# Eight token buffers instead of four, with seven of the eight token tiles made by GpSimd in the attention stage

## The reference

```
h = token_mixer(x)                          # embedding, attention in 192 features, MLP, 2 layernorms
h = h + attention(layernorm(h))             # 12 heads of 16, rms-normed q and k
h = h + soft_moe(layernorm(h))
# soft_moe, for each group of 64 tokens:
xn      = l2norm(x) * sqrt(192) * gamma_in            # the "tokens"
logits1 = xn @ phi.T                                  # 64 tokens x 128 slots
disp1   = softmax over the tokens;  comb1 = softmax over the 128 slots
slots   = disp1.T @ xn;  yn = l2norm(slots) * sqrt(192) * gamma2
# then slot means, second slots, second dispatch, 8 x 4 small MLPs, and back:
out     = comb1 @ out2
```

## Time and profile before

| | |
|---|---|
| runs | 577.52, 575.09, 577.10 us, median 577.1 |
| profiled execution | span 575.4 us from the first to the last instruction; the page gives no separate time for it |
| attention block ends, first slots begins | about 272.6 us |
| first slots ends, second slots begins | about 336.3 us |
| PE busy | 538.0 us, 93% of the span |
| DVE, ACT, POOL busy | 315.0, 257.0, 82.7 us |
| mean granted TensorE clock | 0.985 of full speed |

### The profile page before, as it was taken

One profiled execution on the slowest core, in us unless ns is written; L12 is line 12 of the kernel. 1 busy time (PEld: TensorE's weight loads), 2 busy tenths in 40 slices (PEclk: granted clock), 3 DMA queues, 4 the chain that ended last, 5 costly groups with the idle time before them and its releaser, 6 DMA issues. The chain is left out here.

```text
span 575.4 us, 13736 instructions
## 1 busy us (share of the span) xinstructions
PE 538.0 (93%) x5529; PEld 440.9 (77%) x5529; DVE 315.0 (55%) x738; ACT 257.0 (45%) x822; POOL 82.7 (14%) x128
## 2 busy tenths in 40 slices
PE   6999999999999999999777799999979999999997
PEld 5888888766556656667546565888869999999986
DVE  2348777766777676652235735366643434444343
ACT  1234345356655576543446637366652323323220
POOL 6380000011104321300341100000000000000000
PEclk9999999999999999999869999999999999999999
DMA  6180000000000000000910023000009999999833
GB/s 239 35 283 2 2 0 2 1 2 1 2 2 2 1 1 2 2 1 1 377 76 2 1 90 117 2 1 2 1 1 381 412 331 315 322 335 337 232 56 117
DMA packets 20722, 58.81 MB, mean 102 GB/s; under 512 B 3042, under 2 KB 9796, under 8 KB 20548
## 3 DMA queue, kind: packets, MB, share of 16 engines
q1 hardware_dynamic: 14756, 49.47, 23.2%
q0 software_dynamic: 1056, 4.33, 4.1%
q10 hardware_dynamic: 4848, 4.13, 2.5%
HBM read 53.21 MB, written 4.33 MB: 100 GB/s over the span
## 5 line engine op out<-in xcount | busy, mean ns | idle before, releaser
L2042 PE MATMUL banks<-slots_t,w 64*128 64x128 f32 x1536 | 94.1, 272 | 1.3 <-PEq L1737 1.1
L2042 PEld LDWEIGHTS banks<-slots_t,w 64*128 64x128 f32 x1536 | 92.6, 188 | 1.9 <-issue 1.6
L1138 DVE TENSOR_REDUCE qk<-banks 128x4 f32<-128x1024 f32 x48 | 58.8, 1226 | 39.5 <-PE banks L601 39.5
L2115 ACT ACTIVATE ex_gelu<-banks,b_sb 128x128 f32<-128x128 f32 x128 | 36.6, 369 | 90.6 <-PE banks L2042 90.6
L601 PE MATMUL banks<-qk_t 16*128 16x256 f32 x384 | 54.3, 400 | 2.6 <-DVE qk L1138 2.4
L608 PE MATMUL banks<-qk_t 17*128 17x256 f32 x384 | 54.4, 400 | 0.0
L2135 DVE SCALAR_TENSOR_TENSOR ex_act_t<-banks,b_sb,ex_gelu 128x128 f32<-128x128 f32 x128 | 36.0, 344 | 29.6 <-ACT ex_gelu L2115 29.6
L2073 PE MATMUL banks<-w,ex_act_t 64*128 64x192 f32 x512 | 49.5, 323 | 1.0 <-DVE ex_act_t L2135 1.0
L601 PEld LDWEIGHTS banks<-qk_t 16*128 16x128 f32 x384 | 33.2, 184 | 20.3 <-issue 13.8
L2073 PEld LDWEIGHTS banks<-w,ex_act_t 64*128 64x128 f32 x512 | 43.4, 187 | 1.2 <-issue 1.2
L2145 DVE TENSOR_REDUCE ex_rows<-banks 128x192 f32<-128x384 f32 x32 | 17.8, 558 | 47.3 <-PE banks L2073 47.3
(11 more groups left out here) (231 smaller groups left out, 1048.4 us busy)
## 6 DMA issues: line engine op xcount, KB each, us to landing
w<-in_w SPq DMA_DIRECT2D x32, 768.0 KB, 11.0
w<-in_w2e SPq DMA_DIRECT2D x32, 384.0 KB, 11.7
w_slot<-in_w_slot SPq DMA_DIRECT2D x8, 576.0 KB, 4.2
rows_scratch<-ex_rows ACTq DMA_DIRECT2D x28, 96.0 KB, 6.9
yn_all<-rows_scratch POOLq DMA_DIRECT2D x7, 384.0 KB, 9.2
out<-h SPq DMA_DIRECT2D x8, 192.0 KB, 1.9
qkv_w_sb<-in_qkv_w SPq DMA_DIRECT2D x1, 864.0 KB, 4.9
wk_t<-in_wk_t ACTq DMA_DIRECT2D x2, 289.5 KB, 3.6
```

The source lines that it names most:

```text
L1138: nc.vector.tensor_reduce(to, flat(MAXES[0], MAXES[1] + 1).rearrange("p (h t n) -> p h t n", h=2, n=SEQ), AX.X, ALU.max, negate=True).then ...
L2042: return nc.tensor.matmul(bank[:, j * P:(j + 1) * P], g.w1[n % BUFS][rows, first + j * P:first + (j + 1) * P], x, start=start, stop=stop, ...
L2115: nc.scalar.activation(gelu[n % 2][:, j * P:(j + 1) * P], gate_bank(n)[:, j * P:(j + 1) * P], ACT.Gelu_apprx_tanh, bias=g.t["b1"][:, n, HB ...
```

## The change

The number of token buffers becomes eight, one per sequence: four of their own as before, and four in one new tile, `late_tokens`. GpSimd makes the tokens of sequence n-3 (not n-4) behind its work for sequence n of the attention bodies, and those of sequences 5 and 6 after the loop; only sequence 7's are made in first slots, at the head of GpSimd's list. The wait on `slots_made` and the one on `weighted` go. `late_tokens` lives to the end of the program, and three later users take their space from it: both `logits` tiles of second dispatch, one `gelu` tile and the four `rows` tiles of the experts.

```diff
@@ mixer_and_attention, GpSimd
-            for s in range(NX):
-                for col in (0, TPS * (DIM + 1) - 1):
+            for s in range(BATCH):
+                for col in (0, TOKENS_LEN - 1):
                     nc.gpsimd.memset(g.tokens[s][:, col:col + 1], 1e-3)
...
-                if n >= 4:
-                    make_tokens(n - 4)
+                if n >= 3:
+                    make_tokens(n - 3)
+            make_tokens(BATCH - 3)
+            make_tokens(BATCH - 2)
@@ first_slots, PE
             def turn(n):
-                if n >= NX:
-                    pe.wait_ge(S["weighted"], n - NX + 1)
+                if n == BATCH - 1:
+                    pe.wait_ge(S["weighted"], 1)
...
-                                               x[n % NX][:, 1 + c * P:1 + (c + 1) * P], g.ident[:, :])
+                                               x[n][:, 1 + c * P:1 + (c + 1) * P], g.ident[:, :])
@@ first_slots, GpSimd
             def make_x(n):
-                count = n - NX
-                if count >= 2:
-                    pool.wait_ge(S["weighted"], count - 1)
...
-                pool.wait_ge(S["centred"], TPS * (count + 1))
-                pool.wait_ge(S["slots_made"], count + 1)
-                nc.gpsimd.tensor_tensor(x[n % NX][:, 1:1 + TPS * DIM].rearrange("p (t d) -> p t d", t=TPS),
+                pool.wait_ge(S["centred"], TPS)
+                nc.gpsimd.tensor_tensor(x[n][:, 1:1 + TPS * DIM].rearrange("p (t d) -> p t d", t=TPS),
...
+            make_x(BATCH - 1)
             for n in range(BATCH):
-                if n + NX < BATCH:
-                    make_x(n + NX)
                 scale_comb(n)
@@ second_dispatch
-        logits = sb("logits", [P, GPS, P])
+        logits = [g.late_tokens[:, u * GPS * P:(u + 1) * GPS * P].rearrange("p (g n) -> p g n", g=GPS)
+                  for u in range(W)]
@@ experts
-        gelu = sb("gelu", [P, HID])
+        gelu = [g.late_tokens[:, 0:HID],
+                ctx.enter_context(nc.sbuf_tensor("ex_gelu1", [P, HID], F32))]
...
-        rows = [ctx.enter_context(nc.sbuf_tensor(f"ex_rows{u}", [P, DIM], F32)) for u in range(ROWS)]
+        rows = [g.late_tokens[:, HID + u * DIM:HID + (u + 1) * DIM] for u in range(ROWS)]
@@ tower
-        g.tokens = [sb(f"tokens{s}", [P, TPS * (DIM + 1)]) for s in range(NX)]
+        own = [sb(f"tokens{s}", [P, TOKENS_LEN]) for s in range(OWN_TOKENS)]
+        g.late_tokens = sb("late_tokens", [P, (BATCH - OWN_TOKENS) * TOKENS_LEN])
+        g.tokens = [tile[:, :] for tile in own] + [
+            g.late_tokens[:, s * TOKENS_LEN:(s + 1) * TOKENS_LEN] for s in range(BATCH - OWN_TOKENS)]
```

More of the change, by code:

```diff
@@ L40 @@
 SLOT_BUFS = 3
-NX = 4
+OWN_TOKENS = 4
+TOKENS_LEN = TPS * (DIM + 1)
 EARLY = 4
@@ L1392, in make_slots @@
                         last = nc.tensor.matmul(g.ps[SLOTS[half]][:, AND_ONE(t)], disp[n % 2][rows, t, :],
-                                                x[n % NX][rows, AND_ONE(t)], start=True, stop=True)
+                                                x[n][rows, AND_ONE(t)], start=True, stop=True)
                 last.then_inc(S["slots_made"], 1)
```

## The result

The changed kernel took 567.98 us (median of 4 runs, 567.29 to 568.48), the kernel before beside it 576.12 us (4 runs, 575.09 to 577.52): a ratio of 0.985, 95% interval 0.982 to 0.987. Forecast were 567.3 us and a range of 565.5 to 572.0. Timed again later, the two took 567.15 and 576.04 us.

The account below looks back on a forecast made before the run. Bound: in first slots PE and GpSimd wait for each other in a circle, and PE's clock falls. Terms 0.90 + 1.75 + 1.37 + 1.11 (waits) + 4.66 (clock) = 9.79 us, so 577.1 - 9.8 = 567.3 us; range 565.5 to 572.

Parts of the forecast that it names:

- The waits: First slots, PE's four waits for GpSimd at turn_comb: 5.13 of 7.1 us go, the rest passes to ACT's copy.
- The waits and the clock in the steps together: First slots, up to comb 4: four steps of 5.37 us without wait or low clock, 9.79 us won (5.13 + 4.66).
- The likeliest course of the clock: First slots: with shorter gaps PE's clock stays at 2.4 GHz, worth 4.66 us beyond the waits; chance 0.50.
- my own signs of being wrong: Clock of 0.5 in first slots; attention bodies over 19.6 us or DVE above 14.66; later first slots; new PE waits.
- one short fall remains: Rival: in first slots one clock fall stays, behind the filling gap, costing at most 1.75 us: 569.1 us; chance 0.25.
- The gap in step 0: First slots, 1.80 us before turn_disp(0): pipeline filling, which stays; whether it alone brings a clock fall isn't shown.
- GpSimd's added work in attention: Three more token tiles of 3.04 us each in the attention stage: cost 0, at most 9.1 us by holding DVE.
- Memsets and sequence 7's tokens: Eight more memsets and 3 us of tokens opening first slots: no cost; at most 0.3 and 3.04 us.
- The shared space: logits, gelu and rows tiles taken from late_tokens: same instructions and waits, cost 0.
- the clock falls as before: Rival: in first slots the clock still falls and only the wait's 5.13 us are won: 572.0 us; chance 0.12.
- The half clock through the block: Rival: PE stays at 1.2 GHz from 284 to 336, 17 us more, 594 us; chance 0.03.
- The DVE contention: Rival: GpSimd's tokens in attention hold DVE, 9.1 us, so 576.4 us and no change; chance 0.03.

Follow-up runs that it names:

- experiment 9: Kernel before, wait kept, with 6 identity matmuls filling each of the four gaps in which PE waits for GpSimd: 572.83 us, ratio 0.994.
- experiment 4: Changed kernel with the wait for make_slots and a token-sized dummy multiply put back ahead of scale_comb(0 to 3): 576.37 us, ratio 0.997.
- experiment 6: Changed kernel with identity matmuls filling PE's gaps at the two ends of first slots: 565.38 us, 1.8 below the changed kernel beside it.
- experiment 1: Kernel before, four token buffers, no tokens moved, with scale_comb(n) put ahead of make_x(n + 4) in GpSimd's list: 570.61 us, ratio 0.987.
- experiments 1, 3 and 4: Of these, 3 is the kernel before with 13 identity matmuls in each of four gaps where PE waits for GpSimd: 582.39 us, ratio 1.009.
- experiment 10: Changed kernel with each of the seven token tiles of the attention stage centred three times over on GpSimd: 569.03 us, ratio 0.986.

## Why the prediction was right

**The waits** (forecast 5.13 us). The owner of the gap changed as worked out: ACT's copy, 0.10 us before PE. Step 0 won 0.91 us against 0.90, both counted from the stage's start.

**The waits and the clock in the steps together** (forecast 5.13 + 4.66 = 9.79). From the stage's start to the fifth `turn_comb` 9.92 us were won; the step is 5.34 against 5.37. This sum was right and for the reason given: experiment 9 takes the falls away and leaves the waits, experiment 4 brings waits and falls back and nearly all of the time.

**The split between the two** was wrong. Counted from the stage's start, the fifth `turn_comb` stands at 40.96 us in the kernel before, at 34.74 with the falls gone and the waits there (experiment 9), and at 31.04 in the changed kernel. So the clock is worth 6.2 us there and the waits 3.7. I had priced each wait beside a PE that was partly at 1.2 GHz, 1.11 to 1.75 us from comb 1 on; at 2.4 GHz it costs 0.99 a step (6.33 against 5.34). The two terms overlap by some 1.5 us, and only their sum came out, since it was taken from a step without either. That experiment 9 won 4.4 us as a whole, near my 4.66, is chance: it is 6.2 less the 1.5 of a fall at its end.

The executions of the kernel before agree. There are 47 in these comparisons, and the mean granted clock gives each its time at 1.2 GHz (span x 2 x (1 - clock)):

```
at 1.2 GHz, us      6.9     10.3     13.8     17.3     20.8
executions            1        9        9       21        7
mean time, us    572.87   574.86   575.86   577.32   578.56
```

A line through the 47 is 570.9 + 0.37 x (us at 1.2 GHz). By it the commonest case, 17.3 us, costs 6.4 us, which is the 6.2 of the traces and not 4.66. Its start, 570.9 with no fall at all, is an estimate beyond the points; experiment 6, the changed kernel with no fall, took 565.38, and 3.7 us of the 5.5 between them are the waits. Of the rest, about 1 us lies in the experts block.

**The likeliest course of the clock** was right in the steps and wrong at the end: "the clock is at 1.00 from 273 to 330" failed at 317.5, and 3.4 us at 1.2 GHz in first slots was the first of my own signs of being wrong. I looked at the gaps that the change shortens and not at two that it leaves, 1.14 us at `turn_means(5)` and 0.81 at `make_slots(7)`. The kernel before has them too, and its profiled execution passed them at 1.00, which I took for proof. Of the thirteen later traces nine have a fall there, and the four without one are those in which these gaps are filled. It cost 1.5 us (first slots 55.2 us long, not 53.9), which is the rival "one short fall remains" at another place than I gave it; its price, at most 1.75, was sound. In the profiled span 0.3 us from before the stage and 1.1 from the experts happened to make up for it, so the agreement to 0.1 us is luck; the medians, -8.1 and -8.9 us, are the fairer measure, and the 9.8 was 0.9 to 1.7 too much. The gap in step 0, of which I had written that it isn't shown to bring a fall alone, does bring one: in the traces of experiments 1, 3 and 4 the clock falls at about 279, one to two microseconds behind it, with no other gap above 0.3 us in the stage until then; in other traces, that of the kernel before among them, it doesn't.

**GpSimd's added work in attention** (forecast 0): right, and with room; experiment 10 adds 28 us more and the bodies keep their length. **Memsets and sequence 7's tokens**: no trace of a cost; `scale_comb(0)` waited 3.44 us for its input behind the tokens. **The shared space** was put at 0 with no row to bound it, and no cost is seen; PE's wait for the DMA out of `rows` is shorter in every trace with the tiles in `late_tokens`, by 0.6 us in the profiled pair.

**The rivals.** That the clock falls as before is refuted by the windows after. The half clock through the block was never seen; 20.8 us was the most in those 47 executions. The DVE contention exists (experiment 10) and is 0.14 us in a body where DVE has idle time. The Trainium skill's rule in *GPSIMD Engine Reference*, section 8, that GpSimd and some VectorE instructions contend for SBUF, agrees with what lengthened: beside GpSimd's centring a DVE instruction that reads and writes SBUF took 18% longer, and reductions out of PSUM did not. Whether it is of the kinds that the rule names, no run here shows. The Trainium skill's rule in *TensorE: Matmul & The Clock Gate*, "A second HAM failure mode: psum-queue depth-cycling", did better than I gave it credit for: where gaps of 1.14 and 0.81 us follow each other at the end of the stage, the clock fell in nine traces of the ten that have them, and in none of the four in which they are filled.

What isn't settled is when such a gap brings a fall. The kernel of experiment 1 had 3.4 us at 1.2 GHz in one execution and some 10.3 in three, with the same program, and I made no run that would tell what decides.

## What to carry to other kernels

A short instruction on which the fast engine waits should not stand in a queue behind one that itself waits for the fast engine; look for such circles in the waits, and first try to swap the two, which here gave the same as four more buffers. Price the step by one of the same loop that already runs without the wait, and name the engine that is late next: here its order was the next 2.3 us. Don't add the price of a wait to the price of the low clock as if they were separate: take both from one step that has neither, or measure one with the other held. Where PE has short gaps, read the granted clock of each, in several executions, and count the gaps that the change leaves beside those that it removes.

## What the hardware showed that I had not expected

A float32 matmul of 128 columns on the identity is two instructions of 0.12 us at 2.4 GHz, so 13 fillers took 3.17 us. By the line through the 47 executions a microsecond at 1.2 GHz cost 0.37 us and not 0.5; that part of PE's slower work lies under other engines' waits would explain it, but isn't shown. The stretches at 1.2 GHz in the traces lasted 3.4, 6.8 or 13.7 us. Filling PE's gaps with useless matmuls, which adds to PE's work, made the kernel 1.8 us faster (experiment 6).
